# The set-up of a state space scan, walked batch by batch instead of step by step

## The reference

```python
xz = x @ W_in
xi, z = jnp.split(xz, 2, axis=-1)                 # 256 channels each
xc = lax.conv_general_dilated(...)                # 4 taps over time, each channel alone
xc = _silu(xc + conv_b)
x_dbl = xc @ W_x                                  # 40 columns
dt, Bm, Cm = jnp.split(x_dbl, [DT_RANK, DT_RANK + D_STATE], axis=-1)   # 8, 16, 16
delta = jax.nn.softplus(dt @ W_dt + b_dt)
A = -jnp.exp(A_log)
dA = jnp.exp(delta[..., None] * A)
dBu = delta[..., None] * Bm[:, :, None, :] * xc[..., None]
def step(h, inp):
    dA_t, dBu_t, C_t = inp
    h = dA_t * h + dBu_t
    y = jnp.einsum('bdn,bn->bd', h, C_t)
    return (h, y)
_, ys = lax.scan(step, h0, ...)                   # over the 1024 tokens
y = ys + xc * D
return y * _silu(z) @ W_out
```

## Time and profile before

| | us |
|---|---|
| median of 3 runs | 2124.43 (2123.16 to 2131.59) |
| the profiled execution | 2116.9 |
| its span, first to last instruction | 2114.9 |
| mixer, first projection to first scan instruction | 1671.24 to 1754.05 |
| mixer, first scan instruction to last weighting | 1754.05 to 1972.37 |

### The profile page before, as it was taken

The page is one execution under the profiler, slowest core; times in us unless marked ns, Lnnn a source line. Parts: engine busy times, 40 slices in busy tenths (PEclk is TensorE's granted clock), DMA queues, the critical chain, the costliest instruction groups (busy, mean ns, idle before and its releaser), DMA issues. The chain is left out here.

```text
span 2114.9 us, 26299 instructions
## 1 busy us (share of the span) xinstructions
PE 1611.9 (76%) x9065; PEld 1007.2 (48%) x9065; DVE 1163.8 (55%) x2598; ACT 688.4 (33%) x1006; POOL 785.9 (37%) x510
## 2 busy tenths in 40 slices
PE   3899999999899999999966677855219455776547
PEld 2555556565655556656542455634217212222437
DVE  5454555545454455554447523666703659999614
ACT  1333333343134333334305322321002344545112
POOL 0544434554155443455400040001052008898324
PEclk9999999999989999999988975966559767989758
DMA  1000000000000000000000000002320211222052
GB/s 50 6 1 5 5 5 5 5 5 1 6 6 6 0 5 5 5 5 0 1 12 1 6 1 8 24 2 101 88 63 19 56 32 70 78 72 70 17 143 69
DMA packets 47259, 55.97 MB, mean 26 GB/s; under 512 B 8817, under 2 KB 34697, under 8 KB 46913
## 3 DMA queue, kind: packets, MB, share of 16 engines
q1 hardware_dynamic: 44272, 49.00, 7.9%
q0 software_dynamic: 2912, 6.02, 0.8%
HBM read 42.85 MB, written 12.15 MB: 26 GB/s over the span
## 5 line engine op out<-in xcount | busy, mean ns | idle before, releaser
L353 POOL TENSOR_TENSOR l0a_acc<-l0a_E 128x1792 f32<-128x1792 f32 x16 | 64.4, 4023 | 440.3 <-ACT l0a_E L425 440.3
L425 ACT ACTIVATE l0a_E<-l0a_ring 128x1024 f32<-128x1024 f32 x192 | 148.9, 810 | 196.6 <-DVE l0a_scrap L817 196.6
L353 POOL TENSOR_TENSOR l0a_acc<-l0a_acc,l0a_E 128x1536 f32<-128x1536 f32 (+2 forms) x96 | 200.8, 2092 | 9.7
L2543 PE MATMUL mx_ysum<-mx_hst,main_ident 128*128 128x512 f32 x256 | 139.9, 681 | 47.3 <-POOL mx_hst L2631 42.0
L2644 POOL TENSOR_TENSOR mx_dBu<-mx_XI,mx_BB 128x1024 f32<-128x1024 f32 x64 | 137.6, 2177 | 80.4 <-DVE mx_XI L2707 80.4
L812 DVE TENSOR_TENSOR l0a_ring<-l0a_ring,l0a_cap 128x256 f32<-128x256 f32 x128 | 55.4, 433 | 197.4 <-PE l0a_ring L553 197.4
L563 PE MATMUL l0a_agg<-l0a_E,l0a_VH 128*64 128x512 f32 (+3 forms) x768 | 154.1, 508 | 0.2 <-ACT l0a_E L425 0.2
L563 PE MATMUL l0a_agg<-l0a_E,l0a_F 128*64 128x512 f32 (+3 forms) x768 | 141.3, 496 | 0.0
L2616 ACT ACTIVATE mx_dA<-mx_DT,mx_A 128x512 f32<-128x512 f32 x128 | 87.9, 690 | 97.0 <-DVE mx_hst L2724 96.9
L2543 PEld LDWEIGHTS mx_ysum<-mx_hst,main_ident 128*128 128x128 f32 x256 | 52.7, 214 | 117.4 <-POOL mx_hst L2631 60.2
L165 PE MATMUL n_turned<-main_ident,n_xn 128*128 128x128 f32 x96 | 25.8, 457 | 91.3 <-DVE n_xn L135 91.3
(11 more groups left out here) (485 smaller groups left out, 3691.4 us busy)
## 6 DMA issues: line engine op xcount, KB each, us to landing
mx_BB<-mx_brows SPq DMA_DIRECT2D x32, 512.0 KB, 3.7
me_W<-in_f_w SPq DMA_DIRECT2D x16, 256.0 KB
l0a_wp<-in_wqkv SPq DMA_DIRECT2D x16, 192.0 KB
moe_Wg<-in_f_wg SPq DMA_DIRECT2D x8, 256.0 KB
moe_Wu<-in_f_wu SPq DMA_DIRECT2D x8, 256.0 KB
moe_Wd<-in_f_wd SPq DMA_DIRECT2D x8, 256.0 KB
moe_Y<-rt_zeros SPq DMA_DIRECT2D x2, 1024.0 KB, 10.8
e_back<-moe_Y SPq DMA_DIRECT2D x8, 256.0 KB, 5.0
```

The lines of the kernel that those rows point to most:

```text
L353: pool.tensor_tensor(dst, src, E[:, :, ecol[jt]:ecol[jt] + w], ALU.add).then_inc(acc_done, 1)
L425: act.activation(E[:, :, at:at + n], pair(k % 2)[:, :, 0:n], ACT.Exp).then_inc(exp_done, 1)
L2543: mm = pe.matmul(ysum[h][:, c * 512:(c + 1) * 512], ident[:, :], hst[:, k % DEEP, c * 512:(c + 1) * 512], start=(n == 0), stop=(n == NS - ...
```

## The change

It rewrites the set-up and leaves the 64 pieces alone.

- Sections are walked batch by batch, (b0,h0), (b0,h1), (b1,h0), (b1,h1), on every engine. ScalarE's list mixes the two batches, and the state products and steps of batch 0 no longer wait for batch 1.
- W_x is one matrix of 40 columns, B, C, then dt: one product set for a batch in place of two.
- dt gets a ninth row of ones and W_dt the bias as a ninth row. The ones are GpSimd's `memset` of the whole tile.
- The rows are copied once, by ScalarE, into `rows4`, 512 tokens to each of the four 32-partition groups. SyncE writes B rows in four DMAs. VectorE splits on 128 x 512, and twelve DMAs carry the parts into `bc`.
- Softplus is ln(1+e) + (max(v,0) - (((1+e)-1) - e)), section by section, with v read from PSUM in place of V: three VectorE instructions and a sum.
- GpSimd starts after the fourth delta, and waits for a section's inflow only ahead of that section's first piece.

```diff
-        loads = ((win, "m_win"), (conv, "m_conv3"), (convb, "m_convb"), (wdt8, "m_wx_dt"), (wbc, "m_wx_bc"), (wdt, "m_wdt"),
-                 (bdt, "m_bdt"), (A, "m_alog3"), (Dp, "m_D"), (wout, "m_wout"), (sel1, "sel32"))
+        loads = ((win, "m_win"), (conv, "m_conv3"), (convb, "m_convb"), (wx, "m_wx"), (wdtb, "m_wdtb"),
+                 (A, "m_alog3"), (Dp, "m_D"), (wout, "m_wout"), (sel1, "sel32"))
...
+        dbl = [work[0], work[2]]
+        zp = [work[1], work[3], work[0], work[2]]
+        sections = [(b, h) for b in range(NB) for h in range(HALF)]
...
+            for b in range(NB):
+                for c in range(2):
+                    g = 2 * b + c
+                    sp.wait_ge(rows_kept, g + 1)
+                    sp.dma_start(brows[:, g * 512:(g + 1) * 512], rows4[32 * g:32 * g + NS, :]).then_inc(brows_out, 16)
+                if b == 0:
+                    sp.wait_ge(brows_out, 32)
+                    for q in range(3):
+                        b_row(q)
+            sp.wait_ge(split_ready, 3)
+            for j in range(3):
+                for g in range(2 * NB):
+                    sp.dma_start(bc[32 * j:32 * j + 32, g * 512:(g + 1) * 512],
+                                 parts4[32 * g:32 * g + 32, j, :]).then_inc(bc_in, 16)
...
+            def state_inputs(b):
+                pe.wait_ge(proj_kept, 5 + 2 * b)
+                for h in range(HALF):
+                    pe.wait_ge(xc_ready, HALF * b + h + 1)
+                    for c in range(2):
+                        mm = pe.matmul(dbl[b][0:2 * NS + RK, c * 512:(c + 1) * 512], wx[:, h, :],
...
+            def steps(b):
+                pe.wait_ge(dt_kept, b + 1)
+                for h in range(HALF):
...
+                        mm = pe.matmul(zp[HALF * b + h][:, c * 512:(c + 1) * 512], wdtb[:, h * P:(h + 1) * P],
...
+            for n in range(6):
+                projected(n)
+            convolved(0)
+            projected(6)
+            projected(7)
+            convolved(1)
+            keep_dt(0)
+            keep_rows(0)
+            convolved(2)
+            decays(0)
+            decays(1)
+            convolved(3)
+            exponents(0)
+            exponents(1)
...
-            pool.wait_ge(du_ready, HALF * NB)
+            pool.memset(dtb[:, :], 1.0).then_inc(pads, 1)
+            pool.wait_ge(dt_ready, HALF * NB)
...
+                if n == 0:
+                    pool.wait_ge(du_ready, HALF * b + h + 1)
...
+            def corrections(n):
+                e = Ex[:, n, :]
+                dve.wait_ge(e_ready, n + 1)
+                dve.tensor_scalar(U(n), e, 1.0, None, ALU.add).then_inc(u_ready, 1)
+                dve.wait_ge(u_ready, n + 1)
+                step.then_wait(dve, dve.scalar_tensor_tensor(e, U(n), 1.0, e, ALU.subtract, ALU.subtract))
+                dve.scalar_tensor_tensor(e, zp[n][:, :], 0.0, e, ALU.max, ALU.subtract).then_inc(z_read, 1)
...
+            corrections(0)
+            corrections(1)
+            delta(0)
+            delta(1)
+            inflow(0)
+            inflow(1)
+            dve.wait_ge(brows_out, 32 * NB)
+            split_rows()
```

More of the change, by code:

```diff
@@ L2477, in _, with b_row @@
         def _(sp):
[L2478 to L2481, removed]
+            def b_row(q):
                 if q >= 3:
@@ L2498, in _ @@
                 mm.then_inc(proj_ready, 1)
-            for b in range(NB):
[L2501 to L2518, removed]
@@ new lines, in convolved, with keep_dt, keep_rows @@
+                act.activation(XC[:, h, seq(b)], XC[:, h, seq(b)], ACT.Silu, bias=convb[:, h:h + 1]).then_inc(xc_ready, 1)
+            def keep_dt(b):
+                act.wait_ge(dbl_ready, b + 1)
+                act.wait_ge(pads, 2)
+                act.activation(dtb[0:RK, seq(b)], dbl[b][2 * NS:2 * NS + RK, :], ACT.Copy).then_inc(dt_kept, 1)
+            def keep_rows(b):
+                for c in range(2):
+                    g = 2 * b + c
+                    act.activation(rows4[32 * g:32 * g + 32, :], dbl[b][0:32, c * 512:(c + 1) * 512], ACT.Copy).then_inc(rows_kept, 1)
@@ new lines, in delta, with inflow @@
+            def delta(n):
+                b, h = sections[n]
+                dve.wait_ge(ln_ready, n + 1)
+                dve.wait_ge(z_read, n + 1)
+                dve.tensor_tensor(DT[:, h, seq(b)], DT[:, h, seq(b)], Ex[:, n, :], ALU.add).then_inc(dt_ready, 1)
+            def inflow(n):
+                b, h = sections[n]
+                dve.wait_ge(dt_ready, n + 1)
+                dve.wait_ge(xc_ready, n + 1)
+                dve.tensor_tensor(du_of(h, b), DT[:, h, seq(b)], XC[:, h, seq(b)], ALU.mult).then_inc(du_ready, 1)
@@ new lines, in split_rows @@
+            def split_rows():
+                dve.wait_ge(rows_kept, 2 * NB)
+                for j in range(3):
+                    if j:
+                        step.then_wait(dve, dve.tensor_tensor(rows4[:, :], rows4[:, :], parts4[:, j - 1, :], ALU.subtract))
+                    dve.tensor_copy(parts4[:, j, :], rows4[:, :]).then_inc(split_ready, 1)
+                    if j < 2:
+                        dve.wait_ge(split_ready, j + 1)
+            corrections(0)
+            corrections(1)
@@ L2702, in _ @@
-            dve.wait_ge(dt_ready, HALF)
-            dve.wait_ge(xc_ready, HALF * NB)
-            for h in range(HALF):
-                for b in range(NB):
-                    c = slice(b * SEQ, (b + 1) * SEQ)
-                    dve.tensor_tensor(du_of(h, b), DT[:, h, c], XC[:, h, c], ALU.mult).then_inc(du_ready, 1)
+            corrections(2)
+            corrections(3)
+            delta(2)
+            delta(3)
+            inflow(2)
+            inflow(3)
             def finish(b, h):
```

147 lines of the change are left out of this document (70 added, 77 removed).

## The result

| | before | after |
|---|---|---|
| timed together first, median of 4 runs | 2123.8 us | 2100.4 us (2090.0 to 2106.5) |
| the same kernels again, 9 and 5 runs | 2129.9 us | 2092.5 us (2089.6 to 2100.1) |
| profiled execution: time, span, granted clock | 2116.9, 2114.9, 0.868 | 2100.8, 2098.7, 0.862 |

The ratio is 0.987 (95% interval 0.985 to 0.990) in the first comparison and 0.983 (0.980 to 0.985) in the second. Forecast were 2098 us and a range of 2087 to 2107.

What follows compares the result with a forecast made beforehand. Bound by the set-up's engine-hopping chain, no engine full: first scan at 1727.1 instead of 1754.05, 26.95 less 0.5 for a slow step product, 26.5 us off the timed median 2124.43, gives 2098 us; range 2087 to 2107.

Steps and rivals of the forecast that it cites:

- first Exp ready: Set-up: Exp of section 0 done at 1698.7 us, some 27.5 us after the first projection.
- corrections of a section: VectorE's softplus corrections: one tensor_scalar and two scalar_tensor_tensor of 1024 columns, 3.41 us per section, 13.6 for four.
- C/B split: VectorE's split of the B and C rows: five instructions on 128 partitions, 2.7 us against 10.2 before.
- Exp to last delta: VectorE's work from first Exp: sum 25.8 us, less 2.3 for the last two inflows; last delta about 1722.4.
- seam: Last delta to first scan: inflows 2 and 3 and dBu 0 block each other and run in turn, 4.7 us.
- slack of the C rows: C rows' DMA path: first C product done at 1723.3, VectorE needs it at 1729.9; slack 6.6 us, cost 0.
- Rival A: At the seam GpSimd and VectorE do not block, TensorE stays at the higher clock: 29.2 us less, 2095; chance 0.15.
- Rival B: TensorE at its lower clock through the step products, 3.62 us each for 1.95: 23.1 us less, 2101; chance 0.22.
- C: The twelve small C-row DMAs land one after the other, delaying the first weighting: 36 us slower, 2161; chance 0.02.
- D: Serial landing at 3.3 to 4 us, or VectorE waiting for ScalarE at every hand-over: 2115 to 2130; chance 0.03.
- Memset at nothing: GpSimd's new 9x2048 memset in the set-up, possibly holding VectorE's cast of `sel`: 0 to 0.3 us, taken as 0.
- One product set: TensorE's state products: one of 40 columns costs what the 32 cost, since 512 streamed columns set a record's time.

Runs made afterwards that it cites:

- early-dBu run: Changed kernel without GpSimd's wait for all four deltas, so dBu starts at the first inflow; first scan 5.2 us later.
- run with the repeated columns: Changed kernel with the 8 step columns computed once more behind the 40-column product, into the same rows; first Exp at 31.25 us, 3.6 later.
- softplus run: Kernel before with only the shorter softplus, one instruction in place of two per half; Exp to scan 31.0 against 33.6 us, 2125.2 us beside 2121.8.

## Why the prediction was right, step by step

All times count from the first projection.

| step | forecast | measured | why |
|---|---|---|---|
| first Exp ready | 27.5 | 27.6 (27.4 to 27.8 in six other runs with fast first projections) | held |
| corrections of a section | 3.41 | 3.13 | taps were the nearest row; a correction takes 0.69, 1.23 and 1.22, not 0.79 and twice 1.31 |
| C/B split | 2.7 | 2.8 | held; the split on 32 partitions costs 7.5 more |
| Exp to last delta | 23.7 | 22.2 | four times 0.28 too much, and 0.4 in the small terms (A's sign, gaps) |
| seam | 4.7 | 4.35 | blocked, but dBu 0 started in the first inflow, not behind the second |
| first scan | 56 | 54.1 (54.7 in the second profile) | the two lines above |
| C rows issued | 5.6 | 7.6 | 0.63 each, not 0.47 |
| last one landed | 3.7 later | 1.8 | priced by loads that spread a row from DRAM over 128 partitions; these go from SBUF to SBUF |
| slack of the C rows | 6.6 | 4.7 | first weighting 1736.34; product done at 1730.6, and ScalarE's copy of 1.0, which the forecast left out, must follow |
| pieces | 219 | 218.6 | held |

**The sum.** 26.5 us forecast, 28.7 found (82.81 and 54.14 from first projection to first scan); the whole mixer is 28.3 shorter. The terms missed by 1.5 between Exp and the last delta (1.1 of it the corrections) and 0.4 at the seam, both to the safe side. The 0.5 taken off for a slow step product was not all needed: the first Exp came 0.2 late.

**Rival A** (no blocking) is refuted by the 4.51 us pair and by the early-dBu run, although its time, 2095, fits the two medians (2100.4 and 2092.5) about as well as mine: the profile, not the time, separates them. **Rival B** was half right: the clock does fall, from the second step product on (2.16 us, then 4.99 for 8 records; in the second profile 2.37 and 6.48). It costs little on the path. The second step product stands ahead of the first Exp, as B says, but it lost only 0.2 to 0.4 us; the first ran in 1.98, and the second batch's products have VectorE's corrections beside them. Before, the same loss stood on the path. **C** is refuted. **D**'s second half, ScalarE's queue holding up VectorE, did not come in this profile, but its margin is thin: VectorE reached its first delta at 1713.33 and its log was done at about 1712.8. In the second profile, with the second batch's products at 6.48, the margin was gone and VectorE waited 0.25 us; the run with the repeated columns waited 3.89.

```profile
1705.97 2.36 DVE L2747 TENSOR_TENSOR mx_DT<-mx_DT,mx_Ex 128x1024 f32<-128x1024 f32 x2 [0.25 <-ACT mx_DT L2642]
```

**Memset at nothing** was right, and for the reason given: VectorE's cast of `sel` did block (2.70 us in place of 1.22), the forecast had priced that case too, and the cast ended 0.3 us before the first tap's input came.

**One product set.** I priced the 40 columns rightly and did not see that one matrix was not needed for it: with the 8 columns in rows 32 to 39 two sets cost no more. That the sets before were serial because both began at row 0 is likely, not shown.

**The part not explained by the stage.** Outside the mixer the executions differ among themselves: the mixer's start lay between 1655.4 and 1668.6 us in the profiles of both kernels and all variants, what follows it between 129.8 and 135.4. In the one pair of profiles this took 12 of the 28 us away. Across the timed runs the gain was 23 us in one comparison and 37 in the other, so that a median within 2.4 us of the forecast is partly luck, and a gain over 35 us, to which the forecast gave 0.02, came up in the second. Within the mixer the kernel before varied by 6.2 us between two profiles, the changed one by 0.4 (296.6 and 297.0). Two causes have names. The set-up before pays for the clock of its long chain of products: first Exp at 49.3, 52.6 and, in the softplus run, 52.6, against 27.4 to 27.8 in seven profiles of the new set-up with fast first projections. So the forecast's rows came from the fastest of three executions of the old set-up up to there. The wait at the start of batch 1 is another 2.2, and it falls on either kernel. Together they put the mixer's gain anywhere from 28.3 to 34.5 us in the profiles at hand; what else makes 23 in one comparison and 37 in the other stays open.

## What to carry to other kernels

When an engine-hopping chain prepares a loop, lay it out per batch so that the second batch's chain runs behind the first one's work on the fullest engine: that was worth 10.6 us here and took most of the products' clock off the path. Then save on that engine: all 128 partitions for a split (7.5 us once the split is on the path), one instruction fewer in the softplus (2.5 us). Start a second engine early only where what it makes is the next thing needed: started 12.5 us earlier, in the middle of VectorE's work, GpSimd cost 5.2 us; at the last delta it gained 0.4. And before a few microseconds between two runs are put down to an edit, look whether the waits that differ lie where the edit is.

## What the hardware showed that was not expected

- A 9x2048 memset on GpSimd stretched a float32-to-bf16 cast on VectorE from 1.22 to 2.70 us, though the memset reads nothing; the first taps behind it ran at 0.75 as always.
- Two products of the same input whose outputs lie in rows 0 to 31 and 32 to 39, 4 records each, took 1.90 us together, as long as one; 8 records put behind, into rows used already, took 3.60 more.
- One and the same wait of VectorE in unchanged code was 1.16 us in six profiles and 2.6 to 3.4 in the other eight, with TensorE's four records just ahead of it at 1.95 us in the six and 3.4 to 3.8 in the eight.
- 32-row, 32 KB transfers cost 0.63 us of SyncE's queue each, and halving them does not halve that.
